# One stack slot per group, rounded and remainder rows in it, turned scores in one pass, scores three steps ahead

## The chip, the cores and the metric

The kernel runs on one core of one Trainium2 chip. The metric is the device time of one execution in microseconds (us); the median of the runs is given. The engines are TensorE (PE in the profile; its weight loads PEld), VectorE (DVE), ScalarE (ACT), GpSimd (POOL) and SyncE (SP), which issues DMAs only.

## What is computed

A Flamingo-like stack of two layers on 16 sequences of 128 tokens with 128 features; the context has 120 tokens a sequence. In short:

```python
x = x + tanh(g_xattn[0]) * attn0(layernorm(x), ctx)   # 16 heads of 8, scale 8 ** -0.5, output projection
x = x + tanh(g_ffn[0]) * moe(layernorm(x))            # 16 experts, best 4 of each token
x = x + tanh(g_xattn[1]) * attn1(layernorm(x), ctx)   # one head of 128
x = x + tanh(g_ffn[1]) * ffn(layernorm(x))            # 128 -> 512, butterflies and gelu, -> 128

# attn0
q = x @ Wq.T + bq; k = ctx @ Wk.T + bk; v = ctx @ Wv.T + bv      # 16 heads
attn = softmax(einsum('bhnd,bhmd->bhnm', q, k) * scale)
out = einsum('bhnm,bhmd->bhnd', attn, v) @ Wo.T + bo
```

The change touches attn0, and the time at which the weights of moe are split.

## The kernel before

Every engine has its own program, written out by hand with semaphores between them; nothing is planned by a compiler. The 16 sequences are four groups of GB = 4.

**Prologue.** TensorE makes keys (keys0, line 859), queries (line 888) and values of the four groups; ScalarE adds the bias and writes them to kt_row and q_rows. VectorE makes the norms of the rows before (normed_rows, line 1308) and then two sums of the identity (lines 1333 and 1334), on which GpSimd waits (line 414) to build the butterfly matrices of the last feed-forward part, up to up_mats (line 424). TensorE needs those for its products (line 1046), which stand between the first half phases of scores.

**Stacks.** The 16 heads lie as four row groups (32 partitions of TensorE each) with four heads in each. A head has 8 features. A stack (stack_k and stack_q, lines 237 to 247) is a copy by DMA, SBUF to SBUF, that puts the 8 features of each head of a row group into the first 8 of its 32 partitions, the four heads side by side in the free dimension. Row 8 of a group of queries gets the negative maximum of each token's scores, row 8 of the keys is 1, all other rows are 0, so that a product over 32 rows gives the score less the maximum. There are two slots, ks[:, g % 2] and qs[:, g % 2]. Groups 0 and 1 are stacked in the prologue by SyncE and ScalarE; groups 2 and 3 by GpSimd in stack(g) (line 454), which waits until the phases of group g - 2 have read the slot and also clears the row of maxima.

**The loop over sequences** (line 1051 on TensorE). phase(b, half) (line 914) issues, in turn, turned scores of sequence b (keys as the weights, L931; ScalarE takes their exponentials, L685) and scores of sequence b + 2 (queries as the weights, L938; VectorE takes each row's maximum, maxima, L1347). Two of the four row groups do the one, two the other. All are fp32, and each fp32 product stands as two records in the trace. There are three PSUM banks for each kind. turn_max(b + 1) (L946) turns the maxima, ScalarE writes them to mxr, and SyncE copies them into the row of maxima (stack_max, line 286), on which the next sequence's phase waits. values(b - 1) (L957), turn_attn(b - 2) (L973), project(b - 2) (L977) and turn_heads(b - 1) (L966) finish earlier sequences; VectorE does weighted (L1354, L1355), residual (L1361) and statistics (L1364). keep_busy (L1003) is a product whose result nobody reads.

**GpSimd beside the loop**: split(q) (line 426) splits a quarter of the expert weights into a rounded and a remainder part (w1_hi, w1_lo) and fetches a later quarter; then the residual base xr (line 442), the down matrices, stack(2), split(2), split(3), stack(3), the up matrix, values1 (line 483), norm2(0) and norm_rows(0) (line 535), whose rows turn_normed(0) (L983) turns on TensorE in sequence 14.

**Mixture of experts** (line 1172): per expert six one-pass fp32r products of 512 columns (L1105 to L1107) and one in fp32 (L1116).

## Time and profile before

| | us |
|---|---|
| median of 3 runs | 356.65 (356.06 to 357.22) |
| the profiled execution, its own time | 356.27 |
| its span in the trace | 354.5 |
| TensorE busy | 314.1 (89%) |
| VectorE busy | 240.3 (68%) |
| ScalarE busy | 211.8 (60%) |
| GpSimd busy | 159.5 (45%) |
| first full phase of the loop starts | 41.35 |
| first product of the experts starts | 134.96 |

The span is the time from the first to the last thing the profiler saw; the time of the execution lies 1.8 us above it. Busy shares are means over stages with different limits, so the two start times say more: prologue, 16 sequences of attention, the rest. Times in the rows further down are us from the start of the span, those with ns are marked in the heading of the view.

### The profile page before, as it was taken

The page shows a single profiled execution, that of the slowest core. Times are in us where ns is not written, and L with a number is a line of the kernel's source. Part 1 is how long each engine was busy: PE and PEld are TensorE (multiplying, and loading weights), DVE is VectorE, ACT ScalarE, POOL GpSimd, SP SyncE. Part 2 cuts the span into 40 slices and gives each one's busy share as a digit, 9 for nine tenths or more (in the row PEclk, how much of TensorE's full clock was granted, in tenths as well). Part 3 has the DMA queues.
Part 4 walks back from the last instruction along what each step waited for, and adds up shares of the span by engine and source line. Part 5 has one row for each costly group of instructions (what it writes and reads, how often), then busy time and mean ns, then how long its engine had stood idle before and what let it go on. Part 6 is the DMA issues. An engine that isn't in the chain of part 4 may idle for free.

```text
span 354.5 us, 7313 instructions
## 1 busy us (share of the span) xinstructions
PE 314.1 (89%) x2654; PEld 222.9 (63%) x2654; DVE 240.3 (68%) x603; ACT 211.8 (60%) x411; POOL 159.5 (45%) x254
## 2 busy tenths in 40 slices
PE   4768998839798998999999978999889998999986
PEld 2435777637677776666666645765656665646866
DVE  5672556625566464969998978788958888758251
ACT  3545366615456576685658666668676566764733
POOL 3358998991998021317936340046200394312020
PEclk9999999969899999999999999999999999999999
DMA  7958220120430004323322223413223332000100
GB/s 232 201 70 186 74 66 4 32 35 4 66 121 7 6 2 138 134 89 112 131 93 87 91 88 86 124 46 108 90 92 115 92 108 97 5 1 3 59 31 30
DMA packets 15091, 27.93 MB, mean 79 GB/s; under 512 B 2552, under 2 KB 4040, under 8 KB 15048
## 3 DMA queue, kind: packets, MB, share of 16 engines
q1 hardware_dynamic: 12720, 23.00, 22.2%
q0 software_dynamic: 1408, 3.18, 4.1%
q10 hardware_dynamic: 928, 1.29, 1.3%
q8 instruction: 21, 0.34, 0.4%
q14 instruction: 14, 0.11, 0.1%
HBM read 24.05 MB, written 1.18 MB: 71 GB/s over the span
## 4 chain that ended last, share of the span: by engine, by line
PE 51%; POOL 14%; DVE 13%; issue 8%; ACT 8%; DMA 5%; SPq 1%; ACTq 0%; DVEq 0%; POOLq 0%
PE bank L1116 10%; PE bank L1105 5%; PE bank L1107 5%; PE bank L1106 5%; PE bank L1226 4%; PE bank L931 4%; PE bank L957 3%; PE bank L1211 3%; DMA x_sb<-in_x 3%; DVE rings L1533 3%; DVE rings L1536 2%; POOL xr L442 1%; POOL w_lo L431 1%; DMA rings<-mxr 1%; ACT rings L792 1%
## 5 line engine op out<-in xcount | busy, mean ns | idle before, releaser
L1105 PE MATMUL bank<-xhl,w_hi 128*128 128x512 f32 x128 | 74.9, 585 | 0.8 <-ACT rings L792 0.8
L792 ACT ACTIVATE rings<-bank,cols 128x512 f32<-128x512 f32 x64 | 44.1, 689 | 49.2 <-PE bank L1107 48.9
L1347 DVE TENSOR_REDUCE nt<-bank 128x4 f32<-128x480 f32 x64 | 39.9, 650 | 40.0 <-PE bank L938 40.0
L1533 DVE SCALAR_TENSOR_TENSOR rings<-rings,gates 128x512 f32<-128x512 f32 x64 | 47.4, 740 | 16.9 <-ACT rings L792 16.6
L1107 PE MATMUL bank<-xhl,w_hi 128*128 128x512 f32 x128 | 50.5, 394 | 0.0
L1106 PE MATMUL bank<-xhl,w_lo 128*128 128x512 f32 x128 | 50.3, 393 | 0.0
L931 PE MATMUL bank<-rings,ks 32*120 32x128 f32 x512 | 38.4, 289 | 10.5 <-DMA rings<-rings 6.4
L796 ACT ACTIVATE rings<-bank,b1c 128x512 f32<-128x512 f32 x64 | 44.0, 688 | 0.5
L931 PEld LDWEIGHTS bank<-rings,ks 32*120 32x120 f32 x512 | 32.3, 186 | 15.9 <-issue 12.4
L938 PE MATMUL bank<-ks,rings 32*128 32x120 f32 x512 | 38.9, 291 | 1.3 <-DVE nt L1347 0.7
L1105 PEld LDWEIGHTS bank<-xhl,w_hi 128*128 128x128 f32 x128 | 24.1, 188 | 18.1 <-ACT rings L792 7.9
L1106 PEld LDWEIGHTS bank<-xhl,w_lo 128*128 128x128 f32 x128 | 24.2, 189 | 17.1 <-issue 14.4
L938 PEld LDWEIGHTS bank<-ks,rings 32*128 32x128 f32 x512 | 32.8, 194 | 2.2 <-DVE nt L1347 1.3
L1116 PE MATMUL bank<-rings,x_sb 128*128 128x512 f32 x64 | 33.1, 598 | 0.0
L1536 DVE TENSOR_SCALAR rings<-rings 128x512 f32<-128x512 f32 x64 | 33.0, 515 | 0.1
L1116 PE MATMUL bank<-wide,x_sb 128*128 128x512 f32 x64 | 32.7, 592 | 0.0
L1107 PEld LDWEIGHTS bank<-xhl,w_hi 128*128 128x128 f32 x128 | 24.0, 187 | 5.7
L533 POOL TENSOR_TENSOR xhl<-xnt,xhl 128x512 fp32r<-128x512 f32 x4 | 5.7, 1422 | 48.3 <-ACT xhl L709 27.1
L1541 DVE TENSOR_TENSOR rings<-rings 128x512 f32<-128x512 f32 x32 | 24.2, 757 | 4.2
L1541 DVE TENSOR_TENSOR wide<-rings 128x512 f32<-128x512 f32 x32 | 22.8, 713 | 4.6 <-DVE rings L1536 0.5
L339 POOL TENSOR_TENSOR cs<-cs,minus_half 128x4 f32<-128x4 f32 (+1 forms) x5 | 7.2, 1437 | 34.9 <-DVE cs L1292 34.9
L685 ACT ACTIVATE wide<-bank 120x512 f32<-120x512 f32 x32 | 17.1, 584 | 6.0 <-PE bank L931 6.0
(247 smaller groups left out, 625.9 us busy)
## 6 DMA issues: line engine op xcount, KB each, us to landing
gates<-gate_rows SPq DMA_DIRECT2D x64, 256.0 KB, 3.1
bw<-in_L_ffn_w POOLq DMA_DIRECT2D x4, 512.0 KB, 5.3
x_sb<-in_x SPq DMA_DIRECT2D x4, 256.0 KB, 7.7
x_sb<-in_L_ffn_w SPq DMA_DIRECT2D x2, 512.0 KB, 4.3
wide<-in_ctx ACTq DMA_DIRECT2D x4, 240.0 KB, 6.8
out<-xr SPq DMA_DIRECT2D x3, 256.0 KB, 2.1
gates<-in_flies SPq DMA_DIRECT2D x1, 704.0 KB, 7.0
rings<-rings POOLq DMA_DIRECT2D x8, 64.0 KB, 4.5
```

Source lines behind the costliest of these rows:

```text
L792: act.activation(esg[:, e % 2, :], SB[1 + e % 2][:, :], ACT.Gelu_apprx_sigmoid, bias=b1_in[:, 0, e:e + 1]).then_inc(s["m_sg"], 1)
L796: act.activation(eb[:, e % 2, :], (SB[3], PK)[e % 2][:, :], ACT.Identity, bias=b1c[:, e:e + 1]).then_inc(s["m_eb"], 1)
L931: mm = pe.matmul(turned_bank(b, gg)[0:M, r * P:(r + 1) * P], ks[32 * gg:32 * gg + 32, i, r, mc], qs[32 * gg:32 * gg + 32, i, r, tc], start ...
L938: mm = pe.matmul(score_bank(ahead, n)[:, r * M:(r + 1) * M], qs[rows32, ia, r, ta], ks[rows32, ia, r, ma], start=True, stop=True)
L1105: pe.matmul(bk[:, :], w1_hi[:, e, branch, :], low(g), start=True, stop=False)
L1106: pe.matmul(bk[:, :], w1_lo[:, e, branch, :], high(g), start=False, stop=False)
L1107: pe.matmul(bk[:, :], w1_hi[:, e, branch, :], high(g), start=False, stop=True).then_inc(s[done], 1)
L1116: pe.matmul(Y[:, :], w2_sb[:, e, :], es[e % len(es)], start=False, stop=(e == E - 1), skip_group_check=True).then_inc(s["m_y"], 1)
L1347: dve.tensor_reduce(nt[:, b % 2, OF[n], :], score_bank(b, n)[:, 0:HR * M].rearrange("p (r m) -> p r m", r=HR), AX.X, ALU.max, negate=True) ...
L1533: dve.scalar_tensor_tensor(eq[:, j, :], esg[:, j, :], GELU_LIMIT, gates[:, (n - 1) % NG, :], ALU.min, ALU.mult).then_inc(s["m_eq"], 1)
L1536: dve.tensor_scalar(ec[:, j, :], eb[:, j, :], LIMIT + 1.0, 1.0 - LIMIT, ALU.min, ALU.max).then_inc(s["m_ec"], 1)
L1541: dve.tensor_tensor(es[e % len(es)], eq[:, j, :], ec[:, j, :], ALU.mult).then_inc(s["m_s"], 1)
```

## The change

- Each group has a stack slot of its own. Groups 0 and 1 lie in the space of the expert weights w1_lo and w1_hi, groups 2 and 3 in ks and in xhl and a new tile qs. kt_row moves into the ring space, and the second attention's p1 and p1t and the buffers hid move to the butterfly matrices' space.
- ScalarE writes keys and queries rounded (fp32r). VectorE computes the remainders from PSUM, low_keys and low_queries: (PSUM + bias) - rounded. TensorE's next keys0 and queries wait for these in place of ScalarE's copy.
- A stack has four rows per feature: queries rounded, remainder, rounded, and one for the maximum or zero; keys rounded, rounded, remainder, and one that is 1 at MAX_ROW. That is three DMAs of 128 rows for keys and three for queries of each group, all on SyncE; those of groups 2 and 3 stand between the first stack_max.
- The turned scores take these rows as fp32r, in one pass. The rows' scores take them as fp32, so they still stand as two records.
- phase(b, half) makes the scores of sequence b + 3. Two more half phases and a second turn_max stand ahead of the loop; the last three sequences have turned scores alone, and there values and turn_attn begin with a keep_busy.
- GpSimd fills the slots of groups 2 and 3 where split(0) and split(1) stood; all four splits come after the turned scores of sequence 7, ahead of values1.

The diff, cut to what the steps speak of:

```diff
+    MAX_ROW = 3
+    AHEAD = 3
...
-        qs = ring_row[:, 0:8 * GT].rearrange("p (i r t) -> p i r t", i=2, r=HR)
+        w1_hi_row = w1_hi[:, :, :, :].rearrange("p e j c -> p (e j c)")
+        w1_lo_row = w1_lo[:, :, :, :].rearrange("p e j c -> p (e j c)")
+        KSLOT, QSLOT = HR * GB * M, HR * GT
+        k_rows = (w1_lo_row[:, 0:KSLOT], w1_lo_row[:, KSLOT:2 * KSLOT], ks[:, 0, :], ks[:, 1, :])
+        q_flat = (w1_hi_row[:, 0:QSLOT], w1_hi_row[:, QSLOT:2 * QSLOT],
+                  xhl[:, :, :].rearrange("p s c -> p (s c)"), qs[:, :])
+        k_slot = [v.rearrange("p (r u m) -> p r u m", r=HR, u=GB) for v in k_rows]
+        q_slot = [v.rearrange("p (r u t) -> p r u t", r=HR, u=GB) for v in q_flat]
+        q_lo = ring_row[:, 0:2 * GT].rearrange("p (i t) -> p i t", i=2)
+        k_lo = ring_row[:, 2 * GT:2 * GT + 2 * GB * M].rearrange("p (i t) -> p i t", i=2)
+        kt_row = ring_row[:, 4 * GT:4 * GT + G * GB * M].rearrange("p (g t) -> p g t", g=G)
...
+        def stacked(eng, slot, row, src, landed):
+            eng.dma_start(slot[row:P:4].bitcast(F32), src).then_inc(s[landed], 16)
...
-            sp.wait_ge(s["ks_fill"], 1)
-            sp.wait_ge(s["kt_rdy"], 1)
-            stack_k(sp, 0, range(HG))
+            def stack_k(g):
+                if g < 2:
+                    sp.wait_ge(s["ks_fill"], g + 1)
+                else:
+                    sp.wait_ge(s["kb_fill"], g - 1)
+                sp.wait_ge(s["kt_rdy"], g + 1)
+                stacked(sp, k_slot[g], 0, kt_row[:, g, :], f"ks_ld{g}")
+                stacked(sp, k_slot[g], 1, kt_row[:, g, :], f"ks_ld{g}")
+                sp.wait_ge(s["kl_rdy"], g + 1)
+                stacked(sp, k_slot[g], 2, k_lo[:, g % 2, :], f"ks_ld{g}")
+
+            def stack_q(g):
+                sp.wait_ge(s["qs_zero"], g + 1)
+                sp.wait_ge(s["qt_rdy"], g + 1)
+                stacked(sp, q_slot[g], 0, q_rows[g], f"qs_ld{g}")
+                stacked(sp, q_slot[g], 2, q_rows[g], f"qs_ld{g}")
+                sp.wait_ge(s["ql_rdy"], g + 1)
+                stacked(sp, q_slot[g], 1, q_lo[:, g % 2, :], f"qs_ld{g}")
+
+            stack_k(0)
             sp.dma_start(flies, a["flies"]).then_inc(s["ld_fly"], 16)
-            sp.wait_ge(s["qs_zero"], 1)
-            sp.wait_ge(s["qt_rdy"], 1)
-            stack_q(sp, 0, range(HG // 2))
-            sp.wait_ge(s["ks_fill"], 2)
-            sp.wait_ge(s["kt_rdy"], 2)
-            stack_k(sp, 1, range(HG))
+            stack_q(0)
+            stack_k(1)
             sp.dma_start(mats[:, W_T, :].rearrange("p (c d) -> p c d", c=HC), a["L1_ffn_W_exp"]).then_inc(s["ld_exp"], 16)
-            sp.wait_ge(s["qs_zero"], 2)
-            sp.wait_ge(s["qt_rdy"], 2)
-            stack_q(sp, 1, range(HG))
+            stack_q(1)
...
-                sp.dma_start(qs[HD:P:32, (b // GB) % 2, :, b % GB * P:(b % GB + 1) * P], mxr[:, b % 2, :]
+                sp.dma_start(q_slot[b // GB][MAX_ROW:P:32, :, b % GB, :].bitcast(F32), mxr[:, b % 2, :]
                              ).then_inc(s[f"mx_ld{b % 2}"], 16)
 
             for b in range(NB):
                 stack_max(b)
+                if b in (0, 2):
+                    stack_k(2 + b // 2)
+                if b in (1, 3):
+                    stack_q(2 + b // 2)
...
+            for g in range(2, G):
+                pool.tensor_copy(k_rows[g], which[:, MAX_ROW:MAX_ROW + 1].to_broadcast([P, KSLOT])).then_inc(s["kb_fill"], 1)
+                pool.memset(q_flat[g].bitcast(F32), 0.0).then_inc(s["qs_zero"], 1)
...
-            split(0)
-            split(1)
...
-            def stack(g):
-                pool.wait_ge(s["ks_fill"], 2)
-                pool.wait_ge(s["kt_rdy"], g + 1)
-                pool.wait_ge(s["qt_rdy"], g + 1)
-                pool.wait_ge(s["st_mm"], (g - 1) * GB * HG)
-                stack_k(pool, g, range(HG))
-                stack_q(pool, g, range(HG))
-                pool.dma_start(qs[HD:P:32, g % 2, :, :], qs[HD + 1:P:32, g % 2, :, :]
-                               ).then_inc(s[f"qs_ld{g}"], 16)
-
-            stack(2)
-            split(2)
-            split(3)
-            stack(3)
...
+            def halves():
+                pool.wait_ge(s["st_mm"], 2 * GB * HG)
+                for q in range(NQ):
+                    split(q)
...
+            halves()
...
             turned_max(0)
             taken("up_mm1", mats[:, HALFWAY, :], PO[:, :], "up_ev1")
+            turned_max(1)
...
-                if b + 1 < NB:
-                    turned_max(b + 1)
+                if b + 2 < NB:
+                    turned_max(b + 2)
...
-                    pe.wait_ge(s["kt_rdy"], g)
+                    pe.wait_ge(s["kl_rdy"], g)
...
-                    pe.wait_ge(s["qt_rdy"], g)
+                    pe.wait_ge(s["ql_rdy"], g)
...
             def phase(b, half):
 
-                ahead = b + 2
+                ahead = b + AHEAD
                 if 0 <= b < NB:
-                    i, mc, tc = rows_of(b)
+                    k_, q_, u = k_slot[b // GB], q_slot[b // GB], b % GB
...
                 if ahead < NB:
-                    ia, ma, ta = rows_of(ahead)
+                    ka, qa, ua = k_slot[ahead // GB], q_slot[ahead // GB], ahead % GB
                     if ahead % GB == 0 and half == 0:
-                        pe.wait_ge(s[f"ks_ld{ahead // GB}"], 16 * HG)
-                        pe.wait_ge(s[f"qs_ld{ahead // GB}"], 16 * (HG + ahead // (2 * GB)))
+                        pe.wait_ge(s[f"ks_ld{ahead // GB}"], 16 * 3)
+                        pe.wait_ge(s[f"qs_ld{ahead // GB}"], 16 * 3)
                     need(pe, "nt_rdy", ahead * HG + 2 * half - 1)
                 for r in range(HR):
                     for j in range(2):
                         if 0 <= b < NB:
                             gg = 2 * half + j
-                            mm = pe.matmul(turned_bank(b, gg)[0:M, r * P:(r + 1) * P], ks[32 * gg:32 * gg + 32, i, r, mc],
-                                           qs[32 * gg:32 * gg + 32, i, r, tc], start=True, stop=True)
+                            mm = pe.matmul(turned_bank(b, gg)[0:M, r * P:(r + 1) * P], k_[32 * gg:32 * gg + 32, r, u, :],
+                                           q_[32 * gg:32 * gg + 32, r, u, :], start=True, stop=True)
...
-                            mm = pe.matmul(score_bank(ahead, n)[:, r * M:(r + 1) * M], qs[rows32, ia, r, ta],
-                                           ks[rows32, ia, r, ma], start=True, stop=True)
+                            mm = pe.matmul(score_bank(ahead, n)[:, r * M:(r + 1) * M], qa[rows32, r, ua, :].bitcast(F32),
+                                           ka[rows32, r, ua, :].bitcast(F32), start=True, stop=True)
...
             def values(b):
 
                 pe.wait_ge(s["exp_rdy"], (b + 1) * HG)
                 pe.wait_ge(s["v_st"], b + 1)
                 need(pe, "on_rdy", b)
+                if b >= NB - AHEAD:
+                    keep_busy(PO, 1)
...
-                pe.wait_ge(s["mxr_rdy"], min(b + 4, NB))
+                pe.wait_ge(s["mxr_rdy"], min(b + 5, NB))
                 need(pe, "x1_rdy", b)
+                if b >= NB - AHEAD:
+                    keep_busy(TP, 1)
...
-            phase(-2, 0)
+            phase(-3, 0)
             queries(2)
...
-            pe.wait_ge(s["qt_rdy"], G)
-            phase(-2, 1)
-            phase(-1, 0)
+            pe.wait_ge(s["ql_rdy"], G)
+            phase(-3, 1)
+            phase(-2, 0)
             pe.wait_ge(s["v_rdy"], 2 * G)
             turn_max(0)
...
             keep_busy(bank[3], 1)
+            phase(-2, 1)
+            phase(-1, 0)
+            turn_max(1)
             phase(-1, 1)
-            pe.wait_ge(s["kt_rdy"], G)
+            pe.wait_ge(s["kl_rdy"], G)
             pe.wait_ge(s["bo_rdy"], 1)
...
                 phase(b, 0)
-                if b + 1 < NB:
-                    turn_max(b + 1)
+                if b + 2 < NB:
+                    turn_max(b + 2)
...
+            def low_keys(g):
+                dve.wait_ge(s["kt_rdy"], g + 1)
+                if g >= 2:
+                    dve.wait_ge(s[f"ks_ld{g - 2}"], 16 * 3)
+                dve.scalar_tensor_tensor(k_lo[:, g % 2, :].bitcast(F32R), bank[4][:, 0:GB * M], bcol[:, CK0:CK0 + 1],
+                                         kt_row[:, g, :], ALU.add, ALU.subtract).then_inc(s["kl_rdy"], 1)
+
+            def low_queries(g):
+                dve.wait_ge(s["qt_rdy"], g + 1)
+                if g >= 2:
+                    dve.wait_ge(s[f"qs_ld{g - 2}"], 16 * 3)
+                dve.scalar_tensor_tensor(q_lo[:, g % 2, :].bitcast(F32R), bank[2][:, :], bcol[:, CQ0:CQ0 + 1],
+                                         q_rows[g], ALU.add, ALU.subtract).then_inc(s["ql_rdy"], 1)
 
...
-            dve.tensor_copy(ks[:, 1, :, :], keys_of).then_inc(s["ks_fill"], 1)
+            dve.wait_ge(s["ld_kb"], 16)
+            low_keys(0)
+            dve.tensor_copy(k_rows[1], keys_of).then_inc(s["ks_fill"], 1)
             for g in range(1, G):
                 row_stats0(g)
             refined(1, GB, rr[:, 0:1, 0:GB])
             normed_rows(0)
             own.wait()
             variances(NB - GB, stats[:, GB:NB, :], mean[:, GB:NB])
+            low_keys(1)
             refined(2, NB - GB, rr[:, 0:1, GB:NB])
-            for g in range(1, G):
-                normed_rows(g)
+            normed_rows(1)
+            low_queries(0)
+            low_keys(2)
+            normed_rows(2)
+            normed_rows(3)
+            low_queries(1)
+            low_keys(3)
...
             maxima(0, 0)
             maxima(0, 1)
+            low_queries(2)
+            low_queries(3)
             row_bias()
             maxima(0, 2)
             maxima(0, 3)
+            for n in range(HG):
+                maxima(1, n)
             for n in range(HG - 1):
-                maxima(1, n)
+                maxima(2, n)
             for b in range(NB + 2):
-                if b + 1 < NB:
-                    maxima(b + 1, HG - 1)
+                if b + 2 < NB:
+                    maxima(b + 2, HG - 1)
                 if b >= 2:
                     weighted(b - 2)
-                if b + 2 < NB:
+                if b + AHEAD < NB:
                     for n in range(HG - 1):
-                        maxima(b + 2, n)
+                        maxima(b + AHEAD, n)
```

## Rows read from the trace of the kernel before

**Rows 1.** The page, one line: granted clock in 40 slices of 8.9 us, tenths.

```profile
PEclk9999999969899999999999999999999999999999
```

**Rows 2.** Stretches of the attention: start:end, length, busy (records) per engine, clock, DMA share, GB/s.

```profile
65.25:82.71 17.46, 10.62 (x204) 8.41 (x205) 6.79 (x17) 6.29 (x19) 14.01 (x15) 0.80 0.19 33
87.62:100.07 12.45, 10.35 (x205) 8.25 (x205) 6.80 (x17) 6.31 (x19) 12.01 (x18) 0.86 0.45 86
```

**Rows 3.** Timeline of a steady sequence: start, duration, what, idle before and its releaser.

```profile
64.44 0.66 DVE L1347 TENSOR_REDUCE nt<-bank 128x4 f32<-128x480 f32 x1 [1.50 <-PE bank L938]
...
65.25 0.34 PE L931 MATMUL bank<-rings,ks 32*120 32x128 f32 x1 [0.21 <-DVE nt L1347]
...
66.88 1.08 PE L957 MATMUL bank<-rings,vst 120*32 120x128 f32 x32 [0.26 <-DVE on L1355]
...
68.15 0.36 PE L931 MATMUL bank<-rings,ks 32*120 32x128 f32 x1
...
69.36 0.66 DVE L1347 TENSOR_REDUCE nt<-bank 128x4 f32<-128x480 f32 x1 [1.50 <-PE bank L938]
```

**Rows 4.** Waits of the first 140 us: total, times, longest.

```profile
PE bank L931 <- DMA rings<-rings: 6.4, 1, 6.4
```

**Rows 5.** The chain that ended last, in order of time: start, duration.

```profile
89.33 4.58 DMA rings<-mxr
```

**Rows 6.** Timeline of the prologue.

```profile
21.59 3.17 DVE L1311 TENSOR_SCALAR rings<-x_sb,mean,rr 128x128 f32<-128x128 f32 x12
...
25.29 0.24 POOL L415 COPY ones_low<-sums 128x64 f32<-128x64 f32 x1 [3.23 <-DVE sums L1334]
...
34.23 1.15 PE L938 MATMUL bank<-ks,rings 32*128 32x120 f32 x16 [0.56 <-ACT rings L643]
...
35.44 1.05 POOL L398 TENSOR_TENSOR mats<-blocks,sums 128x512 f32<-128x512 f32 x1
...
36.12 1.15 PE L938 MATMUL bank<-ks,rings 32*128 32x120 f32 x16 [0.74 <-DVE nt L1347]
...
37.32 1.06 PE L1022 MATMUL bank<-mats 128*128 128x128 f32 x8
...
38.74 1.15 PE L938 MATMUL bank<-ks,rings 32*128 32x120 f32 x16
...
40.82 0.60 PE L1003 MATMUL bank<-wt,ident 128*128 128x256 f32 x2
...
41.35 0.36 PE L931 MATMUL bank<-rings,ks 32*120 32x128 f32 x1
```

**Rows 7.** Groups of VectorE, whole span: count, busy us, mean ns, idle before.

```profile
L1524 DVE SCALAR_TENSOR_TENSOR xr<-bank,tg,xr 128x512 f32<-128x512 f32 x3 | 2.3, 751 | 1.3 <-PE bank L1226 1.1
```

**Rows 8.** DMA issues, whole span: count, size of one, median us from issue to landing.

```profile
ks<-kt_row POOLq DMA_DIRECT2D x8, 60.0 KB, 3.7
```

**Rows 9.** Stretch inside the first refill of the slots, columns as in rows 2.

```profile
72.00:73.00 1.00, 0.00 (x0) 0.00 (x0) 0.00 (x0) 0.00 (x0) 1.00 (x3) 1.00 1.04 127
```

**Rows 10.** DMA queues from 60 to 80 us: packets, MB, share of 16 engines.

```profile
q0 software_dynamic: 416, 0.54, 15.7%
```

**Rows 11.** Timeline of the last sequences of the attention.

```profile
120.90 0.60 PE L983 MATMUL bank<-ident,xn 128*128 128x128 f32 x4
...
126.19 1.14 PE L931 MATMUL bank<-rings,ks 32*120 32x128 f32 x16
...
132.78 1.08 PE L957 MATMUL bank<-wide,vst 120*32 120x128 f32 x32 [0.56 <-DVE on L1355]
```

**Rows 12.** Timeline of the experts, two one-pass products that follow one another.

```profile
165.31 0.40 PE L1105 MATMUL bank<-xhl,w_hi 128*128 128x512 f32 x1
165.54 0.39 PE L1106 MATMUL bank<-xhl,w_lo 128*128 128x512 f32 x1
```

**Rows 13.** Stretches of GpSimd: split(2) and split(3); then values1 to norm_rows(0).

```profile
72.84:79.86 7.02, 3.54 (x57) 3.05 (x61) 1.22 (x2) 1.11 (x3) 6.79 (x5) 0.55 0.16 14
100.98:114.58 13.60, 12.41 (x285) 9.66 (x277) 8.94 (x22) 8.68 (x25) 12.61 (x21) 1.00 0.14 44
```

53 lines of the change are left out of this document (19 added, 34 removed).

## The prediction

> **What bounds the kernel now.** I read the page first: TensorE's granted clock is full in nearly all of the 40 slices; it drops around the two places that the next views name [rows 1]. The cut by stretches [rows 2] then gives the stages: a prologue up to 41.35 us, the sixteen sequences of the first attention, and from 134.96 us on the mixture of experts and what follows, 219.5 us, whose work the change leaves alone. So the question is when the first expert's product starts.
>
> Within the attention three things set that moment.
> - The steady sequence takes 4.92 us: the reduction of the third score bank starts at 64.44 and at 69.36 us [rows 3]. The loop is mixed. That reduction (0.66 us) ends and phase(b,0) starts at 65.25; VectorE goes on with residual, statistics, the fourth reduction, reciprocal and the division by it, and the values start at 66.88, 0.26 us after TensorE had nothing else; 68.15 is phase(b,1), whose end releases the next reduction. TensorE's own gaps are only those 0.21 and 0.26 us.
> - Two stalls at the changes of group. The waits name the refill of the two stack slots, 6.4 us once [rows 4], and the chain a DMA of the maxima that takes 4.58 us behind the other refill [rows 5]. TensorE is at half clock behind each (means 0.80 and 0.86 [rows 2]). The first covers two sequences from 65.25 to 82.71, 17.46 us for 2 x 4.92 = 9.84, a loss of 7.6; the second from 87.62 to 100.07, 12.45 us, a loss of 2.6. Together 10.2 us.
> - The prologue's critical chain is GpSimd's: VectorE's sums done by 25.2, GpSimd from 25.29, its matrix done at 36.49, TensorE's products at 37.32, the first full phase at 41.35 [rows 6].
>
> **Removed: the stalls, -10.2 us.** Each group gets its own slot, so no stack waits for an earlier group's phases. Groups 2 and 3 are stacked by SyncE between the first maxima, behind GpSimd's new fills (some 2 us each). With the start worked out below, the fills end by about 43.9 and 47.8 us, the twelve DMAs are issued by 60 us, and the ninth sequence's scores are wanted some 25 us after the first full phase. What is late next there: the maxima's DMA of sequence 1 stands in SyncE's queue behind three stacks and is issued near 48 us instead of 43; the third step ahead pays for it, since the reader is then at 55 us. So I cost this at nothing.
>
> **Added: the prologue, +8.5 us.** VectorE gets eight subtractions from PSUM. The nearest row is 0.75 us for 128x512 with a PSUM operand [rows 7]. Four of them (two of queries, two of keys, about 2.9 us) now stand between the rows' norms and the sums, so these end at 28.1 at least instead of 25.2. The fourth, low_keys(3), also reuses the buffer that the stack of keys 1 reads, so it waits for that stack's third DMA. SyncE issues the third DMA of queries 0 only when VectorE has made their remainder (the norms of group 1 begin at 21.59 and take a third of 3.17 us [rows 6], plus 0.75: 23.4 us), then keys 1, some 0.7 us each: last issue at 25.6. A stack's DMA takes 3.7 us from issue to landing in the trace [rows 8], which gives 29.3; then 0.7 and 0.6 us: sums at 30.6, 5.4 us later than now. GpSimd's 11.2 us follow unchanged: matrix at 41.9. On TensorE phase(-3,1) waits for the last query remainder, near 35.8 us, and phase(-2,0) ends at 39; both are covered by that wait. From the products: 1.4 us to phase(-2,1), 1.9 us (the distance of two half phases that wait for a reduction, 34.23 to 36.12 [rows 6]) to phase(-1,0), 1.9 to phase(-1,1), and 2.6 from there to the first full phase as now (38.74 to 41.35). 42.0 + 1.4 + 1.9 + 1.9 + 2.6 = 49.8 us, against 41.35: +8.45.
> Bounds. If the wait for keys 1 costs nothing, sums are 2.9 us late and the start is 47.3: +6.0. The stacks now carry three copies, 1.5 MB a group. If they move at the 127 GB/s at which the refills saturate the DMA engines [rows 9], the three of queries 0 and keys 1 end near 32.5, those of queries 1 near 41, and the start comes to 53.1: +11.8. I take the middle because the packets of a refill, 416 in 15.7% of 16 x 20 us, took 121 ns each [rows 10], so that 384 packets of three DMAs over 16 engines need some 3 us.
> A rule here: the Trainium skill, "DMA: Bandwidth & Descriptors", section "Why a DMA increments its semaphore by 16 and not by 1", says a DMA runs on the largest number of engines up to 16 that divides the outermost sizes of both sides. The old stacks have 8 rows at one end, the new ones 32 and 128. By that rule the new ones spread over twice the engines, and the sum would go by the lower bound, 2.5 us less than mine; the trace has no such transfer.
>
> **The phases: 0 in the loop.** Before, a full half phase has 32 matmul records, a half phase of scores alone 16, of turned scores alone 16. All take the same: 1.15 us for scores alone [rows 6], 1.14 for turned alone [rows 11], and 1.1 for both in the loop, 68.15 to the reduction at 69.36 [rows 3]. The row groups run side by side, and a phase is as long as one row group's four fp32 products. The change halves the turned half of the records and leaves the rows' scores in fp32: the phase stays. The 4.92 us also stay because the order of reductions, shifted by one sequence, is the same.
>
> **The end of the attention: -0.3 us.** Sequences 13 to 15 now have turned scores alone. A one-pass product of 512 columns starts every 0.23 us (165.31, 165.54 [rows 12]), so 128 columns are 0.06 to 0.11 us, and a half phase takes some 0.65 instead of 1.14. Sequence 13 has no reductions: 3.8 instead of 4.92, -1.1. Sequence 14: two half phases save 1.0, one keep_busy costs 0.53 (40.82 to 41.35 [rows 6]): -0.5. Sequence 15 is VectorE's (values wait for the division, 132.78 [rows 11]); there two keep_busy stand open: +1.1. If 128 columns in one pass are no quicker than in fp32, the three are -0.5, +0.5, +1.1. GpSimd now splits the expert weights after sequence 7: start at 88.4, two of them take 7.0 us in the trace [rows 13], four with two issues and their DMAs 16.4, so 104.8; then as now from 100.98 to 114.58, 13.6 us [rows 13]: rows ready at 118.4. TensorE wants them at 120.90 [rows 11] - 41.35 - 10.2 + 49.8 - 1.1 = 118.1. It waits about 0.2 us; 1.5 at most, if the weights land slowly. Sum -0.3, from -0.5 to +2.6.
>
> **Sum.** -10.2 + 8.45 - 0.3 = -2.0 us on the span of 354.5, so 352.5. The profiled execution took 356.27, the median of the runs is 356.65; the difference applied to the median gives 354.6 us. 0.3% of it, 1.07 us, is about what a measurement of this kernel can tell from no change. Bounds: -10.2 + 6.0 - 0.5 = -4.7 (352.0) and -10.2 + 11.8 + 2.6 = +4.2 (360.9).
>
> **Rivals.**
> - The stacks stay slow. Then the prologue takes +11.8: -10.2 + 11.8 - 0.3 = +1.3, 358.0 us. For it: 1.04 of the engines' time for 127 GB/s [rows 9]. Against: those refills wrote eight neighbouring partitions each, the new ones spread over all. Between this and the forecast the outcome is no change.
> - Slower: the one-pass products don't run beside the fp32 ones of the other row groups. The place is each mixed half phase. Eight products at 0.23 x 128/512 = 0.0575 us add 0.46 us; phase(b,1) stands on the loop, phase(b,0) has 0.26 us of cover [rows 3], so 0.66 us a sequence, 13 times: +8.6, 363.2 us. It decides as soon as the added time passes 0.26 in one half and anything in the other. Against: one-pass and fp32 products alternate in the experts without loss.
> - The phase is bound by the number of records. Then 24 instead of 32 shorten 0.87 us by 0.22, 13 to 26 times: -2.9 to -5.7, about 350.5. Against: 16 records take as long as 32.
> - The change doesn't do what it says, the stalls only move to the maxima's DMA behind the new stacks. One such wait cost some 2.6 us more, the loss of the second stall [rows 2, 5]: 357.2 us. The third step ahead speaks against it. The Trainium skill, "DMA: Bandwidth & Descriptors", section "Queues, rings and completion order", states the ground of this rival: each DMA engine takes the descriptors of one queue in their order.
>
> **How the numbers follow.** Forecast 0.53 (0.44 faster, 0.09 within), slow stacks 0.18 (half within, half slower), no side by side 0.15, records 0.09, moved stall 0.05. Faster 0.53, same 0.23, slower 0.24. Range 350.8 to 359.5: it leaves out the second rival and a part of the third.
>
> **What would show it.** No idle of TensorE over 1 us between sequences 4 and 13, clock full there; reductions still 4.92 us apart; the first full phase near 49.8 us with VectorE's sums near 30.6; the first expert's product near 133. Wrong, if the distance of the reductions moves, if the first full phase is beyond 52 us, or if TensorE waits for GpSimd's rows in sequence 14.

## The result, and the profile after

Five executions of the changed kernel took 360.89, 364.55, 371.35, 389.44 and 400.76 us, median 371.35; the kernel before took 357.22 (356.06 to 359.20). The forecast was 354.6, between 350.8 and 359.5. The two quickest are 1.017 times the kernel before (95% 1.009 to 1.025), the middle one 1.04 times. The executions of this one program differ in TensorE's mean granted clock: 0.967, 0.953, 0.935, 0.872 and 0.842 in the order of their times. From the ends that is 39.87 us for 0.125, or 3.2 us for each 0.01. Continued to the 0.986 of the profiled execution before, the line reaches 354.8 us, a hint, and no more, that the counting was right and the clock was not in it. The experiments test this.

The profiled execution is the one of 400.76 us, span 398.9, the clearest case of what went wrong. Its page, busy shares and granted clock in 40 slices of 10 us, the answer to [rows 1]:

```profile
PE   5785899999999999999999999699997999899987
PEclk9999555555555555799999999999999999999999
```

From 40 to 160 us TensorE is busy 90% or more in each slice but one and the clock stands at 5, which is 1.2 GHz of 2.4. The stretches say it without rounding (columns as in [rows 2]):

```profile
33.00:36.00 3.00, 1.52 (x19) 1.15 (x17) 1.40 (x4) 0.69 (x1) 2.69 (x7) 1.00 0.70 259
36.00:38.00 2.00, 1.36 (x17) 1.06 (x17) 1.32 (x3) 0.00 (x0) 1.61 (x8) 1.00 0.03 12
38.00:40.00 2.00, 0.05 (x1) 0.05 (x1) 1.01 (x2) 0.27 (x1) 1.78 (x5) 0.73 0.01 4
40.00:42.00 2.00, 2.00 (x9) 2.00 (x10) 0.00 (x0) 0.00 (x0) 2.00 (x2) 0.50 0.01 4
53.00:165.00 112.00, 111.61 (x1174) 88.48 (x1174) 45.34 (x102) 46.15 (x128) 49.78 (x73) 0.50 0.10 35
```

The fall comes after a thin stretch of the new prologue. Its timeline, the answer to [rows 6]:

```profile
28.37 0.28 DVE L1368 TENSOR_REDUCE sums<-ident 128x8 f32<-128x128 f32 x1
...
34.71 1.15 PE L942 MATMUL bank<-w_lo,w_hi 32*128 32x120 f32 x16 [1.34 <-DVE rings L1304]
...
36.61 1.15 PE L942 MATMUL bank<-w_lo,w_hi 32*128 32x120 f32 x16 [0.74 <-DVE nt L1381]
...
39.95 2.08 PE L1031 MATMUL bank<-mats 128*128 128x128 f32 x8 [1.98 <-POOL mats L415]
```

Eight products that took 1.06 us before take 2.08 here: from here on TensorE's work costs about double. A sequence of the loop, by two successive values (L970):

```profile
79.93 1.94 PE L970 MATMUL bank<-rings,vst 120*32 120x128 f32 x32
...
87.67 1.94 PE L970 MATMUL bank<-wide,vst 120*32 120x128 f32 x32
```

7.74 us, where [rows 3] has 4.92. The 44.4 us between the two spans then lie as follows: the first full phase starts at 53.28 instead of 41.35 (+11.9), from it to the first expert's product (179.0) it takes 125.7 instead of 93.6 (+32.1), and after that 219.9 instead of 219.5. The stalls of [rows 4, 5] are gone: from 54 to 165 us TensorE's waits for another engine add up to 0.4 us. They can't be seen in the time, since a TensorE at 1.2 GHz is the bound of everything. Two of the signs of being wrong that were named beforehand came true: the first full phase is beyond 52 us, and the distance from one sequence to the next moved.

### The profile page after: what moved, and what is told of

Same layout as the page of the kernel before. It is cut to its first block, busy times and chain, and to the rows that moved or that the text cites. A ratio compares the mean times of both kernels' runs of the same rounds, so it can differ in the third digit from the quotient of the medians.

```text
span 398.9 us, 6836 instructions
## 1 busy us (share of the span) xinstructions
PE 366.8 (92%) x2410; PEld 263.1 (66%) x2410; DVE 247.6 (62%) x611; ACT 214.0 (54%) x411; POOL 156.1 (39%) x240
## 3 DMA queue, kind: packets, MB, share of 16 engines
q10 hardware_dynamic: 848, 1.15, 0.9%
## 4 chain that ended last, share of the span: by engine, by line
PE 68%; DVE 10%; ACT 7%; issue 7%; POOL 4%; DMA 2%; SPq 0%; ACTq 0%; DVEq 0%; POOLq 0%
PE bank L942 10%; PE bank L1128 9%; PE bank L970 7%; PE bank L1117 5%; PE bank L1119 5%; PE bank L1118 5%; PE bank L935 5%; PE bank L1238 4%; PE bank L1223 3%; PE bank L992 2%; DMA x_sb<-in_x 2%; DVE rings L1571 2%; PE bank L956 2%; PE bank L1031 1%; DVE rings L1574 1%
## 5 line engine op out<-in xcount | busy, mean ns | idle before, releaser
L1381 DVE TENSOR_REDUCE nt<-bank 128x4 f32<-128x480 f32 x64 | 39.9, 651 | 69.2 <-PE bank L942 69.2
L942 PE MATMUL bank<-w_lo,w_hi 32*128 32x120 f32 x256 | 30.3, 406 | 3.3 <-DVE nt L1381 1.9
L942 PEld LDWEIGHTS bank<-w_lo,w_hi 32*128 32x128 f32 x256 | 26.1, 297 | 5.0 <-DVE nt L1381 2.7
L700 ACT ACTIVATE mxr<-bank 16x128 fp32r<-16x128 f32 x16 | 4.3, 268 | 43.0 <-PE bank L951 43.0
L935 PE MATMUL bank<-w_hi,w_lo 32*120 32x128 f32 x128 | 23.5, 427 | 0.2 <-ACT wide L691 0.2
L691 ACT ACTIVATE rings<-bank 120x512 f32<-120x512 f32 x32 | 17.1, 585 | 11.2 <-PE bank L935 11.2
```

The source lines that it names most:

```text
L935: mm = pe.matmul(turned_bank(b, gg)[0:M, r * P:(r + 1) * P], k_[32 * gg:32 * gg + 32, r, u, :], q_[32 * gg:32 * gg + 32, r, u, :], start=T ...
L942: mm = pe.matmul(score_bank(ahead, n)[:, r * M:(r + 1) * M], qa[rows32, r, ua, :].bitcast(F32), ka[rows32, r, ua, :].bitcast(F32), start=T ...
L1381: dve.tensor_reduce(nt[:, b % 2, OF[n], :], score_bank(b, n)[:, 0:HR * M].rearrange("p (r m) -> p r m", r=HR), AX.X, ALU.max, negate=True) ...
```

## The experiments

Theory A: a thin prologue takes the clock down, and the loop with one-pass turned scores doesn't bring it back. (By thin I mean short of work: TensorE busy 1.52 of 3 and 1.36 of 2 us.) Theory B: the thin prologue is the whole cause. Rival C: a disturbance from outside. All times below are medians of 6 or 12 executions, with lowest and highest and, where the executions are even, the ratio to the kernel before on the same chip, in brackets its 95% interval.

### The kernel again, and three ways to hold the clock

again is the changed kernel unaltered. prologue_filled puts ten products that nobody reads where TensorE stood idle. turned_fp32 takes the one pass back. loop_filled spreads the two products of the last sequences over all.

```diff
 # prologue_filled
+            keep_busy(bank[3], 2)
             pe.wait_ge(s["ql_rdy"], G)
             phase(-3, 1)
+            keep_busy(bank[3], 1)
             phase(-2, 0)
+            keep_busy(bank[3], 1)
...
+            keep_busy(bank[3], 4)
             pe.wait_ge(s["up_mats"], 1)
...
             phase(-2, 1)
+            keep_busy(bank[3], 1)
             phase(-1, 0)
             turn_max(1)
+            keep_busy(bank[3], 1)
             phase(-1, 1)
 # turned_fp32
-    k_[32 * gg:32 * gg + 32, r, u, :], q_[32 * gg:32 * gg + 32, r, u, :]
+    k_[32 * gg:32 * gg + 32, r, u, :].bitcast(F32), q_[32 * gg:32 * gg + 32, r, u, :].bitcast(F32)
 # loop_filled
-                if b >= NB - AHEAD:
-                    keep_busy(PO, 1)
+                keep_busy(PO, 1)
```

(loop_filled does the same with keep_busy(TP, 1).)

> The changed kernel unaltered. In its profiled execution the granted clock fell to 0.50 at 39 us and stood there until 165 us, and over five executions the mean clock lay between 0.842 and 0.967 with 400.8 to 360.9 us. Theory A (with the turned scores in one pass TensorE, once at 1.2 GHz, does not come back to 2.4 GHz during the attention, save by luck): again times spread over 358 to 402 us, falling with the mean clock, at roughly 3.3 to 3.6 us for each 0.01 of it. Rival C (the first five executions were disturbed by something outside the kernel): times within 0.5% of each other, near 355 us, mean clock 0.98 or more.

> The changed kernel with ten products of 128x256 that nobody reads in the idle spots of TensorE between 33 and 48 us (the 1.3 us before the second low-half scores, the 2.0 us before the up matrix). Theory B (the sparse prologue is what takes the clock down at 39 us; without that the attention runs at 2.4 GHz): clock 1.00 from 36 to 120 us, mean 0.98 or more, 351 to 356 us. Theory A (the one-pass scores can't hold or regain the clock): the drop comes later, at one of the first sequences of the loop, or still at 39 us, the mean clock again varies between 0.84 and 0.97, 360 to 400 us.

> The changed kernel with the turned scores read in full fp32 again, over the same stacked rows and three sequences ahead; everything else as changed. Theory A: the clock may still fall at 39 us, but comes back to 1.00 within the first two sequences of the loop; mean clock 0.97 or more, 352 to 358 us, little spread between executions. Theory B: the clock falls at 39 us as before and stays at 0.50 through the loop in most executions, 360 to 400 us or more, since the work of the loop at the lower clock is then even longer.

> The changed kernel with its two products of 128x256 that nobody reads (one ahead of the values, one ahead of the turn of the attention) in every sequence instead of the last three. Theory A: the added products give back some of what the one-pass scores took; the clock falls at 39 us but comes back in the loop in more executions, mean clock 0.95 or more, at a price of 0 to 1 us for each sequence at full clock: 355 to 370 us. Theory B: no help once the clock is down, 362 to 405 us.

- again: 394.27 us (363.11 to 400.18), as uneven as before, while eleven executions of the kernel before on the same chip took 353.97 to 359.48. Rival C falls.
- prologue_filled: 357.35 (355.04 to 357.82), ratio 1.0005 (0.995 to 1.006). It is 1.35 us above what theory B was given.
- turned_fp32: 359.19 (358.71 to 365.07), ratio 1.008 (1.002 to 1.013). It is 1.2 us above what theory A was given.
- loop_filled: 375.33 (370.99 to 380.42), ratio 1.042. Even, but dear: its sequences are 5.98 us apart (values at 82.63 and 88.61). I had expected 355 to 370, since I gave the added pair 0 to 1 us; it costs 1.07, thirteen times. That misses the time, and hits the clock.

The clock lines of their pages, in this order (prologue_filled, turned_fp32, loop_filled):

```profile
PEclk9999999999999769999999998999999999999999
```

```profile
PEclk9999669999999999999999998999999999999999
```

```profile
PEclk9999559999999999999999999999999999999999
```

In the last two the clock falls in the prologue all the same and is back within the first two sequences of the loop; in prologue_filled it doesn't fall there. So the kernel needs both to lose 40 us: a fall, and a loop that doesn't undo it. Theory B falls with turned_fp32, where the prologue is as thin as in the changed kernel. Theory A stands as it is put above. The expectation of prologue_filled had it stronger, that the one-pass loop can't hold the clock either; that is false, the clock is 1.00 from 28 to 115 us there. One more thing shows: prologue_filled has a new dip near 115 us (below).

The profile of again, whose first full phase starts at 51.10, shows that the clock can fall twice before the loop (columns as in [rows 2]):

```profile
40.00:45.00 5.00, 4.25 (x33) 3.42 (x33) 1.22 (x2) 0.60 (x1) 5.00 (x4) 0.69 0.42 149
45.00:50.00 5.00, 4.47 (x37) 3.95 (x34) 2.44 (x4) 0.56 (x3) 5.00 (x5) 0.65 0.40 150
50.00:55.00 5.00, 5.00 (x38) 4.14 (x38) 1.22 (x2) 1.82 (x4) 4.34 (x13) 0.50 0.03 9
```

The clock is down by 37 us, back at 1.00 from 44 to 46, and down again from 47 on. turned_fp32 does the same, 1.00 from 43 to 46 and 0.50 from 47 on, and comes back at 53 us, in the loop; again stays at 0.50 to 160 us. The second fall comes after waits of 0.75 and 0.53 us (0.54 in turned_fp32) for the reductions ahead of three half phases; two of these three are there only for the third step ahead.

### Is it the one gap of 2 us? Can the prologue be made shorter?

gap_filled keeps only the four products ahead of up_mats. sums_early moves VectorE's two sums, for which GpSimd waited 6.95 us, ahead of its wait for the second inverse root; it adds no product (the place is later than the expectation says, at the same 18 us or so). filled_fp32 joins prologue_filled and turned_fp32. sums_early_fp32 joins sums_early, full fp32 and three of the products, the two and the one around phase(-3, 1), not the five that its expectation counts.

```diff
 # sums_early
+            own.mark(dve.tensor_reduce(in_block, ...))
+            dve.tensor_reduce(of_block, ...).then_inc(s["sums_rdy"], 1)
             refined(2, NB - GB, rr[:, 0:1, GB:NB])
...
             low_keys(3)
-            own.mark(dve.tensor_reduce(in_block, ...))
-            dve.tensor_reduce(of_block, ...).then_inc(s["sums_rdy"], 1)
```

> Both edits together: the ten products that nobody reads in the prologue, and the turned scores in full fp32. With the idle filled the first phase of the loop began at 47.2 us; with fp32 the loop took 85.8 us from there to the first expert product, some 1.4 us of it at 1.2 GHz in its first sequence. Theory A (the one-pass scores are what lets the clock fall again in the last three sequences, and the gap what takes it down at 39 us): clock 1.00 from 36 to 140 us, first expert product at 131 to 132 us, 353 to 354 us. Rival (the two ways save the same thing once): 356 to 357.5 us.

> The changed kernel with only four products of 128x256 ahead of the wait for the up matrix, where TensorE stood idle for 2 us until 39.9 us. Theory 'the gap' (that wait alone takes the clock down): as with all ten, 355 to 358 us, clock 0.98. Theory 'the sparse stretch' (TensorE is busy for 1.2 of 3 us from 33 us on, and of 2.7 of 4 us after; no single gap counts): the clock still falls between 35 and 50 us in most executions and the loop stays at 1.2 GHz in some, 358 to 400 us.

> The changed kernel, its turned scores in one pass, with VectorE's two sums (that GpSimd's matrices wait for, and TensorE behind them) ahead of its third group of statistics, at about 18 us instead of 28 us; no products added. The up matrix should be there by 33 to 35 us, and the 2 us wait at 38 us gone. Theory 'the gap': the clock stays at 1.00, the first phase of the loop begins at 45 to 46 us, 352 to 356 us. Theory 'the sparse stretch': the other gaps (1.3 us before 34.7, 0.7 us twice) suffice, the clock falls near 40 us and the time is uneven again, 358 to 400 us.

> The candidate for the fastest: sums ahead as in the run before, turned scores in full fp32, and nine of the ten products that nobody reads less the four ahead of the up matrix. Theory A: clock 1.00 throughout the attention, first phase of the loop at 45 to 46 us, first expert product at 129.5 to 131 us, 351.5 to 353 us. Rival (something else than the up matrix, the reductions, sets the first phase of the loop): as filled_fp32, 353 to 354 us.

- filled_fp32: 354.98 (354.22 to 356.09), ratio 0.990 (0.986 to 0.995). The first expert's product is at 133.7 us, where theory A had 131 to 132.
- gap_filled: 361.77 (360.92 to 366.38), ratio 1.008.
- sums_early: 384.27 (360.61 to 405.12).
- sums_early_fp32: 362.59 (359.62 to 363.66), ratio 1.010, some 9 us above the rival's 353 to 354.

In gap_filled the clock is down before the gap begins:

```profile
33.80 1.15 PE L942 MATMUL bank<-w_lo,w_hi 32*128 32x120 f32 x16 [1.34 <-DVE rings L1305]
35.70 2.06 PE L942 MATMUL bank<-w_lo,w_hi 32*128 32x120 f32 x16 [0.74 <-DVE nt L1382]
37.69 0.38 PE L951 MATMUL bank<-ident,nt 128*16 128x128 f32 x1
37.86 3.62 PE L956 MATMUL bank<-wt,ident 128*128 128x256 f32 x8
```

The second group of scores already takes 2.06 us. So the 2 us gap is not needed for the fall; it comes after waits of 1.34 and 0.74 us with 1.15 us of work between. The clock is back at about 43 us and holds (1.00 from 45 to 50 us), where again fell a second time. That fits the even times; that the four products are what made the difference was not tested by itself.

sums_early gave a surprise. The up matrix was made at 32.4 us instead of 39.9, yet the loop began later. GpSimd also fetches 2 x 512 KB of expert weights behind the sums, and that now fell on the stacks. TensorE's first scores, and the stretch after them:

```profile
28.26 1.80 PE L942 MATMUL bank<-w_lo,w_hi 32*128 32x120 f32 x16 [2.00 <-DMA w_hi<-rings]
```

```profile
28.00:33.00 5.00, 4.74 (x21) 3.31 (x22) 1.45 (x3) 0.69 (x1) 4.38 (x12) 0.56 1.04 402
```

and the time from issue to landing of the key stacks, in the changed kernel and here:

```profile
w_lo<-rings SPq DMA_DIRECT2D x6, 240.0 KB, 3.5
```

```profile
w_lo<-rings SPq DMA_DIRECT2D x6, 240.0 KB, 6.2
```

The DMA engines are full (1.04), the stacks take 6.2 us instead of 3.5, TensorE waits 2.0 us and the mean clock of the stretch is 0.56. My expectation had priced VectorE's and GpSimd's part and no DMA. sums_early_fp32 has the same start (stacks 5.9 us, clock 0.66 from 28 to 33 us), then a second stretch at 0.50 from 45 to 55 us, and its first full phase only at 54.30.

### The end of the attention, the third step, the fetches

tail_fp32 is prologue_filled with full fp32 in the last three sequences only. ahead_two is filled_fp32 with the rows' scores two steps ahead. fetch_late is filled_fp32 with the sums early, the two fetches behind the up matrix and one product ahead of it instead of four. ahead_two_fetch_late joins the last two.

```diff
 # tail_fp32
+                    if b >= NB - AHEAD:
+                        k_, q_ = k_.bitcast(F32), q_.bitcast(F32)
 # ahead_two
-    AHEAD = 3
+    AHEAD = 2
...
-            phase(-2, 1)
-            keep_busy(bank[3], 1)
-            phase(-1, 0)
-            turn_max(1)
-            keep_busy(bank[3], 1)
             phase(-1, 1)
...
-                if b + 2 < NB:
-                    turn_max(b + 2)
+                if b + 1 < NB:
+                    turn_max(b + 1)
```

(The half phases ahead of these are numbered one higher: phase(-3, 0) becomes phase(-2, 0), and so on. ahead_two sets turned_max, maxima and the bounds of x1_rdy and mxr_rdy to match, as in the kernel before.)

> The changed kernel with the ten products in the prologue, and the turned scores in full fp32 in the last three sequences alone (one pass in the other thirteen). With one pass everywhere the clock fell at 115 us, after TensorE had waited 1.25 us for GpSimd's normed rows, and stood at 1.2 GHz for most of 116 to 130 us, and the first expert product was at 135.8 us. Theory A (the last three sequences with one pass leave TensorE too little to do): the clock stays at 1.00 there, first expert product at 131.5 to 132.5 us, 353.5 to 355 us, as filled_fp32. Rival (the one-pass scores of the sequences before weigh too): the clock falls near 115 us again, 356 to 358 us.

> filled_fp32 with the rows' scores two steps ahead instead of three (stacks for each group, full fp32, the products in the prologue as far as their places are left). Two phases of the prologue and one turn of maxima fall away from between 42 and 48 us. Theory D (the third step earns nothing, since a sequence takes 4.9 us with either, and costs its prologue): first phase of the loop at 44.5 to 46 us, sequences 4.9 us apart, 350.5 to 353 us. Rival (three ahead gives the maxima's chain and DMA the time that it needs with stacks for each group): sequences of 5.1 us or more, 355 us or more.

> filled_fp32 with VectorE's sums at 18 us and GpSimd's two fetches of 512 KB behind the up matrix instead of behind the sums; one product that nobody reads ahead of the up matrix instead of four. In the run with the sums alone moved, the stacks' DMAs landed in 6.2 us instead of 3.5 and the first scores waited until 28.2 us instead of 26.9. Theory E (that was the two fetches beside the stacks): stacks land in 3 us again, first phase of the loop at 46 to 47 us, 352.5 to 354 us. Rival (the reductions set the prologue's end): as filled_fp32, 354.5 to 355.5 us.

> The two last together: two steps ahead, sums early, fetches late. By theories D and E: first phase of the loop at 43 to 44.5 us, 349 to 351.5 us. If only D holds: as ahead_two. If the prologue's gaps take the clock down again: 353 us or more.

- tail_fp32: 355.01 (353.31 to 359.56), ratio 0.995 (0.992 to 0.998).
- ahead_two: 351.52 (349.53 to 351.78), ratio 0.984 (0.979 to 0.989).
- fetch_late: 361.32 (359.98 to 363.28), ratio 1.012.
- ahead_two_fetch_late: 356.32 (355.08 to 359.65), ratio 0.999.

The end first. The stretch there in prologue_filled, then in filled_fp32:

```profile
115.00:130.00 15.00, 13.40 (x119) 10.18 (x116) 5.28 (x31) 6.70 (x17) 3.19 (x4) 0.66 0.01 1
```

```profile
113.00:130.00 17.00, 16.54 (x232) 13.50 (x231) 7.37 (x39) 11.21 (x28) 6.33 (x9) 1.00 0.01 2
```

The one-pass end has nearly half the records to do, stands idle more, waits once for GpSimd's rows and falls to 0.66:

```profile
116.37 1.10 PE L998 MATMUL bank<-ident,xn 128*128 128x128 f32 x4 [1.25 <-POOL xn L529]
```

From the first full phase to the first expert's product it takes 88.6 us (47.23 to 135.8), the fp32 kernel 84.9 (48.82 to 133.7), tail_fp32 85.0 (48.60 to 133.6). In these profiles the quicker instructions lose 3.7 us. Two of prologue_filled's six executions took 355.0 and 355.1 us at a mean clock of 0.995, so they seem to have escaped most of it. tail_fp32 has its first expert's product 2.2 us before prologue_filled, although its first full phase came 1.4 us later, and its clock is 1.00 from 100 to 134 us; so the rival, that the thirteen sequences before weigh too, is not borne out by the profiles. The ratios alone, 0.995 and 1.0005, have intervals that overlap.

The third step earned nothing, as theory D had it. ahead_two has its first full phase at 42.99 us, earlier than I thought, and the first expert's product 84.6 us later. It is 3.5 us under filled_fp32 by the medians, 2.3 by the ratios. (ahead_two has eight of the ten products.)

fetch_late missed by some 8 us, ahead_two_fetch_late by 5. Theory E held as far as it went: the key stacks land in 3.6 us, TensorE's first scores no longer wait for a stack (27.74 us, behind other work), and the up matrix was there at 30.7 us. But then, GpSimd and VectorE (start, duration, what):

```profile
34.08 1.82 POOL L445 MEMSET xhl<- 128x2048 f32 x1
35.83 1.79 POOL L444 CAST ks<-which 128x1920 fp32r<-128x1920 f32 x1
37.55 1.81 POOL L445 MEMSET qs<- 128x2048 f32 x1
```

```profile
35.40 4.05 DVE L1379 TENSOR_SCALAR rows<-rows,tg 128x128 f32<-128x128 f32 x1
39.48 0.35 DVE L1381 SCALAR_TENSOR_TENSOR rows<-bank,tg,rows 128x128 f32<-128x128 f32 x1
```

A step of VectorE that takes 0.28 us elsewhere lies for 4.05 us beside three fills of GpSimd and ends 0.09 us after the last. Behind it stand the reductions, and TensorE waits 3.13 us (4.83 in ahead_two_fetch_late) and comes back at 1.2 GHz. The Trainium skill, "SBUF — State Buffer", section "SBUF: two separate sides", says that GpSimd and some operations of VectorE share a port pair as an exclusive lock, and that the other "fully blocks". The trace agrees, and adds that the wait outlasts one instruction: it covers two more that GpSimd issues back to back.

### What is the third step's part, and what do the stacks alone give

fills_late is ahead_two_fetch_late with GpSimd's four fills behind its wait for bo_rdy, which VectorE gives after the step that was blocked. two_one_pass is ahead_two with one-pass turned scores. two_unfilled is ahead_two without the added products: the stacks for each group alone. two_unfilled_one_pass is the changed kernel with two steps ahead and nothing else.

```diff
 # fills_late
-            for g in range(2, G):
-                pool.tensor_copy(k_rows[g], ...).then_inc(s["kb_fill"], 1)
-                pool.memset(q_flat[g].bitcast(F32), 0.0).then_inc(s["qs_zero"], 1)
...
             pool.wait_ge(s["bo_rdy"], 1)
+            for g in range(2, G):
+                pool.tensor_copy(k_rows[g], ...).then_inc(s["kb_fill"], 1)
+                pool.memset(q_flat[g].bitcast(F32), 0.0).then_inc(s["qs_zero"], 1)
```

> As ahead_two_fetch_late, with GpSimd's four fills of the third and fourth group's slots moved behind its wait for the row bias. In ahead_two_fetch_late VectorE's 128x128 step on the bias row (0.28 us elsewhere) lay for 4 us beside those fills, and the reductions and TensorE behind it waited 4.8 us. Theory F (VectorE's step waits for GpSimd's fills): that step takes 0.3 us again, the up matrix is there at 30 to 31 us, first phase of the loop at 41 to 41.8 us, 349 to 350.5 us. Rival (the wait comes from something else on that stretch): the step stays long, 355 to 357 us.

> ahead_two with the turned scores in one pass in every sequence. Theory A: the loop up to its last sequences is the same (4.9 us each), and in the last two the clock falls, as it did with three ahead: first expert product 2 to 4 us later than in ahead_two, 353 to 356 us. Rival (the fall at the end belongs to three steps ahead, whose last three sequences have no row scores, and two such sequences are too few): as ahead_two or up to 1.5 us faster, 350 to 351.5 us.

> The stacks for each group alone: two steps ahead, the turned scores in full fp32, no products added in the prologue. Theory A: the clock falls at 36 to 40 us and is back by 50 us, as in turned_fp32; first phase of the loop at 43.5 to 46 us, 352.5 to 355 us. Rival (with two steps ahead the prologue is dense enough): clock 1.00, as ahead_two, 350 to 352 us.

> The changed kernel with two steps ahead instead of three, nothing else. Theory A (sparse prologue takes the clock down, one-pass scores keep it there): uneven times, 355 to 400 us, the mean clock between 0.84 and 0.97 as in the changed kernel. Rival (it takes the third step's longer prologue and its emptier end as well): all executions within 1% of each other, 351 to 357 us.

- fills_late: 349.78 (348.41 to 351.03), ratio 0.979 (0.975 to 0.983), the lowest of all. Its first full phase is at 43.65 us; I had 41 to 41.8.
- two_one_pass: 351.59 (349.56 to 353.06), ratio 0.984 (0.979 to 0.988).
- two_unfilled: 351.54 (351.17 to 356.69), ratio 0.985 (0.981 to 0.989).
- two_unfilled_one_pass: 350.82, 350.85, 351.32, 398.56, 350.79, 398.25.

In fills_late the step is short again:

```profile
35.42 0.28 DVE L1373 TENSOR_SCALAR rows<-rows,tg 128x128 f32<-128x128 f32 x1
```

Theory F is shown: moving four fills is worth 6.5 us against ahead_two_fetch_late, 7.0 by the ratios. A gain over ahead_two is not shown: it is 1.7 us by the medians, from different chips, and the intervals of the ratios, 0.979 and 0.984, overlap.

two_one_pass is as fast as ahead_two by ratio. The fall at the end that I expected did not come: in its profile the clock is 1.00 there and the first expert's product is 84.4 us after the first full phase. So with two steps ahead the one pass alone doesn't bring that fall, and my rival was right there. A smaller one can come all the same: two_unfilled, with full fp32, shows 0.77 and 0.89 from 120 to 130 us.

two_unfilled answers the question of the heading. With two steps ahead, full fp32 and no product added it takes 351.54 us, ratio 0.985, where ahead_two with eight products has 0.984. So what is left of the change, the slots for each group above all, is worth some 5.5 us, and beside two steps and full fp32 the added products give nothing that can be told. Its profile is of its slowest execution, 356.69 us, and shows the fall of theory A: 0.50 from 38 to 47 us, first full phase at 47.12. The other five took 351.2 to 352.0 us at a mean clock of 0.985 and have no profile. That is below theory A's time, and the clock is not the rival's 1.00.

two_unfilled_one_pass is the sharpest picture of the cause. Six executions of one program took 351 or 398 us and nothing between. In the profiled execution of 350.82 us the clock fell and came back:

```profile
33.00:36.00 3.00, 1.37 (x18) 1.19 (x20) 2.22 (x5) 0.05 (x1) 2.61 (x8) 0.89 0.40 157
36.00:40.00 4.00, 3.05 (x21) 2.54 (x22) 1.52 (x3) 0.27 (x1) 3.54 (x9) 0.50 0.01 2
40.00:45.00 5.00, 5.00 (x46) 3.90 (x48) 1.22 (x2) 1.48 (x4) 5.00 (x4) 0.78 0.42 149
45.00:50.00 5.00, 5.00 (x74) 4.38 (x70) 2.45 (x4) 2.75 (x9) 5.00 (x5) 1.00 0.30 104
```

Here it is back at about 42 us, before the first full phase at 44.65, so this profile doesn't show a one-pass loop undoing a fall. The 398 us have no profile, but their mean clock is 0.828 against 0.985, and they are what a loop at 1.2 GHz gives: 47.5 us more, against 44.4 in the changed kernel's profiled execution. With full fp32 the same prologue stayed within 351.2 to 356.7. Two of six against none of six would be thin by itself. With three steps 8 of 11 executions (the changed kernel and again) lie above 365.07, the slowest of turned_fp32.

The profiles say it more plainly. In three of them a loop with one pass and nothing added begins at the low clock (the changed kernel, again, sums_early), and all three stay at 0.50 until 160 us or later. In four a loop with full fp32 or with two more products a sequence begins there (turned_fp32, loop_filled, sums_early_fp32, two_unfilled), and all four are back at 1.00 within two sequences. So with the one pass the loop stays down, and with more work for TensorE it doesn't. The third step adds its phases to the prologue (47.23 us against 42.99 in the kernels where the clock held), with them the place of the second fall, and, with one pass, the longer dip at the end.

## Why the prediction was wrong

**The step that failed** is one that the working doesn't have. It priced every gap of TensorE at its length and all work at the full clock. The view of the granted clock was read at the two stalls, where it was low and came back by itself [rows 1, 2], and was carried over to a kernel that gives TensorE other work. I had written down the gap myself: phase(-2,0) ends at 39, the up matrix comes at 41.9. The waits near it, and whether the loop behind it would bring the clock back, were not asked. In the changed kernel's profiled execution, at 1.2 GHz, 13 sequences cost 2.8 us each more (7.74 for 4.92); that alone is 37 us. Even the quickest execution, 360.89 us at a mean clock of 0.967, is outside the range. No chance was given to any of this.

**Stalls, -10.2: right.** In filled_fp32, whose clock is 1.00 from 28 to 130 us, the values are 4.91 to 4.92 us apart through both changes of group, and TensorE's longest wait between 49 and 113 us is 0.5 us:

```profile
59.60 1.08 PE L970 MATMUL bank<-wide,vst 120*32 120x128 f32 x32
64.51 1.08 PE L970 MATMUL bank<-rings,vst 120*32 120x128 f32 x32 [0.26 <-DVE on L1395]
...
103.85 1.08 PE L970 MATMUL bank<-rings,vst 120*32 120x128 f32 x32 [0.26 <-DVE on L1395]
108.76 1.08 PE L970 MATMUL bank<-wide,vst 120*32 120x128 f32 x32 [0.26 <-DVE on L1395]
```

The moved stall, a rival at 0.05, is false.

**Prologue, +8.45: too high, the lower bound was right.** The sums ended at 28.65 us in the changed kernel, not 30.6; the matrix at 39.9, 11.2 us after GpSimd's start, as counted. With the gaps filled the first full phase started at 47.23 (+5.9; my bound +6.0), at 48.6 to 48.8 in the two kernels whose profiles have a stretch of low clock before it. The mis-sized term is the wait of low_keys(3) for a stack: 1.02 us, where the sum had 2.5 (30.6 less 28.1). Its last DMA was issued by 25.6 us as forecast, and VectorE went on at 27.46 instead of 29.3:

```profile
27.46 0.72 DVE L1297 SCALAR_TENSOR_TENSOR rings<-bank,cols,rings 128x480 fp32r<-128x480 f32 x1 [1.02 <-DMA w_lo<-rings]
```

That the lower bound fits to 0.1 us is partly luck, since it has this wait at nothing. The slow stacks, the rival at 0.18, are false too. The lower bound was also the one that the Trainium skill's rule in "DMA: Bandwidth & Descriptors", section "Why a DMA increments its semaphore by 16 and not by 1", gave; the result agrees with it, though no run here shows how many engines a stack used.

**Phases, 0: right.** A mixed half phase takes 1.09 us with one-pass turned scores and with fp32 ones:

```profile
100.38 0.28 PE L935 MATMUL bank<-xhl,ks 32*120 32x128 f32 x1 [0.20 <-DVE nt L1387]
...
101.47 0.28 PE L951 MATMUL bank<-ident,nt 128*16 128x128 f32 x1
```

```profile
100.37 0.34 PE L935 MATMUL bank<-xhl,ks 32*120 32x128 f32 x1 [0.21 <-DVE nt L1381]
...
101.46 0.28 PE L951 MATMUL bank<-ident,nt 128*16 128x128 f32 x1
```

(prologue_filled, then turned_fp32). Neither rival on them, that one-pass products don't run beside the others (+8.6) or that the count of records bounds the phase, is true. It also means that the one pass had nothing to give in thirteen of sixteen sequences; it took away work that TensorE could do for nothing.

**End of attention, -0.3: wrong sign with one pass.** 93.6 - 10.2 leaves 83.4 us from the first full phase to the first expert's product; prologue_filled took 88.6, so +5.2. The half phases took 0.63 us as forecast (0.65), TensorE waited 1.25 us for GpSimd's rows (I had 0.2, at most 1.5; that it waits at all was also on my list of signs of being wrong, against my own sum), and then the clock fell, which was not in the sum. With fp32 there it is +1.5, near the +1.1 that I gave as the other bound.

Put together at a nearly full clock: the forecast's span was 352.5, filled_fp32 has 353.9 and a median of 354.98 against my 354.6. That it comes so near is partly luck: filled_fp32 is another kernel, its first full phase is 1.0 us before the forecast's 49.8, and its end of attention 1.8 us longer. The stalls and the phases were read rightly; the state of TensorE's clock outweighed them.

The Trainium skill, "TensorE: Matmul & The Clock Gate", section "What's actually happening", says that "the default state is throttled, and activity releases the throttle". Weighed beforehand, with [rows 1, 2] as its only witness, that sentence would have called the loop safe, as long as activity is read as being busy: it keeps TensorE busy without a break. The trace disagrees with that reading: 111.61 of 112 us busy at 0.50.

**Still open.** What in the one-pass loop keeps the clock at its lower level is not shown: the runs show only that full fp32, or two more products a sequence, made six executions of a kernel even, within 2.6% of each other, where one pass alone spread over 10% and more. Nor is it shown why some executions come off better: none of them was profiled with three steps ahead, and with 360.9 to 390 us and mean clocks of 0.967 to 0.868 they lie between. Of the places in the thin prologue only the one ahead of the up matrix was filled by itself.

## What to carry to other kernels

When a change takes work from TensorE or thins its schedule, read the granted clock as a term of the sum: ask where it could fall, and whether the work behind that place brought it back in the trace. Quicker instructions that shorten nothing on the path are not free. Look at several executions before trusting one, since the same kernel can take 351 us or 398. And when a producer is moved earlier, move with it in thought everything that is queued behind it: here first two fetches, then four fills each cost more than the move gained.
